# GpSimd makes the product of the gate and the state difference

## The reference

```python
h = relu(layernorm(x));  x = x + adj @ (h @ W0) + b0         # layer 0
h = relu(layernorm(x))                                       # layer 1
for _ in range(5):
    m  = adj @ h                                             # m_in = m_out, one matrix
    z  = sigmoid(m @ (w3 halves summed) + h @ u3 + biases)
    r  = sigmoid(m @ (w4 halves summed) + h @ u3 + biases)
    hv = tanh(m @ (w5 halves summed) + (r * h) @ u5 + biases)
    h  = (1 - z) * h + z * hv                                # = h + z * (hv - h)
x = x + h
```

## Time and profile before

| | |
|---|---|
| Median of 3 runs | 1661.34 us (1660.52 to 1661.93) |
| Profiled execution, its own time | 1661.44 us |
| Its span, first to last instruction | 1659.6 us |
| Mean granted TensorE clock | 0.988 of full speed |
| Busy: PE, DVE, ACT, POOL | 96%, 73%, 50%, 14% |

### The profile page before, as it was taken

How to read it: one execution, slowest core, us unless ns; L and a number is a source line. 1 busy time by engine, 2 the same in 40 slices (tenths; PEclk the granted TensorE clock), 3 DMA queues, 4 the chain that set the end, 5 groups by cost and what they waited for, 6 DMA issues and landing times.

```text
span 1659.6 us, 23908 instructions
## 1 busy us (share of the span) xinstructions
PE 1588.5 (96%) x7439; PEld 733.9 (44%) x7439; DVE 1206.0 (73%) x2311; ACT 833.9 (50%) x1298; POOL 226.4 (14%) x548
## 2 busy tenths in 40 slices
PE   5899999999999999999999999999999999999997
PEld 4444444444444444444444444444444444444443
DVE  6577677777777767776777767777768776787677
ACT  3455545455545554545545454455544555454554
POOL 4130020300213002130021201121020300200000
PEclk8999999999999999999999999999999999999998
DMA  3011111111211111111111111211111111111112
GB/s 141 26 26 36 28 39 51 32 32 29 47 38 38 25 38 38 51 25 38 25 38 51 35 28 32 59 30 32 28 35 63 25 25 38 25 38 26 38 26 51
DMA packets 179414, 63.30 MB, mean 38 GB/s; under 512 B 173504, under 2 KB 174272, under 8 KB 179392
## 3 DMA queue, kind: packets, MB, share of 16 engines
q1 hardware_dynamic: 177664, 62.43, 15.8%
q10 hardware_dynamic: 1728, 0.59, 0.1%
HBM read 13.18 MB, written 8.39 MB: 13 GB/s over the span
## 4 chain that ended last, share of the span: by engine, by line
issue 73%; POOL 12%; PE 10%; DVE 2%; DMA 1%; ACT 1%; POOLq 1%; SPq 0%; DVEq 0%
PE ps_m L503 6%; POOL y L400 4%; POOL h_lo L409 2%; DMA adj_in<-in_adj_dram 1%; POOL newton L328 1%; POOL mean L304 1%; POOL rstd L332 1%; POOL newton L318 1%; POOL var_eps L301 1%; POOL newton L330 1%; PE ps_u L510 1%; PE ps_u L512 1%; PE ps_u L511 1%; POOL gap L303 1%; POOL gap L314 0%
## 5 line engine op out<-in xcount | busy, mean ns | idle before, releaser
L503 PE MATMUL ps_m<-adj_hi,nh_hi 128*128 128x512 f16 x1536 | 584.7, 381 | 26.0 <-DVE nh_lo L897 24.4
L503 PE MATMUL ps_m<-adj_lo,nh_hi 128*128 128x512 f16 x1536 | 584.4, 380 | 0.0
L503 PE MATMUL ps_m<-adj_hi,nh_lo 128*128 128x512 f16 x1536 | 584.2, 380 | 0.0
L503 PEld LDWEIGHTS ps_m<-adj_hi,nh_hi 128*128 128x128 f16 x1536 | 150.6, 98 | 211.2 <-ACT nh_hi L670 30.5
L503 PEld LDWEIGHTS ps_m<-adj_hi,nh_lo 128*128 128x128 f16 x1536 | 150.7, 98 | 183.1 <-issue 3.3
L503 PEld LDWEIGHTS ps_m<-adj_lo,nh_hi 128*128 128x128 f16 x1536 | 150.7, 98 | 175.3 <-issue 2.0
L903 DVE SCALAR_TENSOR_TENSOR m_lo<-ps_m,m_hi 128x512 f16<-128x512 f32 x192 | 131.3, 687 | 127.4 <-ACT m_hi L705 127.4
L705 ACT ACTIVATE m_hi<-ps_m 128x512 f16<-128x512 f32 x192 | 112.3, 589 | 196.8 <-PE ps_m L503 196.8
L912 DVE SCALAR_TENSOR_TENSOR cand<-cand,h 128x512 f32<-128x512 f32 x160 | 118.6, 759 | 121.3 <-ACT cand L717 121.3
L736 ACT ACTIVATE h_hi<-h 128x512 f16<-128x512 f32 x158 | 97.3, 630 | 215.4 <-DVE h L924 215.4
L1008 DVE SCALAR_TENSOR_TENSOR rh<-ps_r,w_inv,hu 128x512 f32<-128x512 f32 x160 | 120.2, 751 | 104.8 <-PE ps_r L512 89.5
(11 more groups left out here) (134 smaller groups left out, 2003.9 us busy)
## 6 DMA issues: line engine op xcount, KB each, us to landing
x_in<-in_x_dram SPq DMA_DIRECT2D x16, 512.0 KB, 3.8
out_dram<-y SPq DMA_DIRECT2D x16, 512.0 KB, 2.7
adj_in<-in_adj_dram SPq DMA_DIRECT2D x8, 512.0 KB, 7.6
nh_hi<-h_hi SPq DMA_TRANSPOSE x128, 2.4
nh_lo<-h_lo SPq DMA_TRANSPOSE x128, 2.4
n_hi<-h_hi SPq DMA_TRANSPOSE x30, 2.4
n_lo<-h_lo SPq DMA_TRANSPOSE x30, 2.4
cand<-in_L_gnn_w_w_dram ACTq DMA_DIRECT2D x3, 128.0 KB, 6.4
```

The costliest lines, as they stand in the source:

```text
L503: last = nc.tensor.matmul(ps_m[half][:, :], a[slot][:, k, :], b[:, k, cols(half)], start=(k == 0 and n == 0), stop=(k == BLOCKS - 1 and n ...
```

## The change

The two multiplies of `new_state_end` go from DVE to POOL, in a function `gate_diff`. POOL's own loop is given up for `pair_schedule`, with `layernorm0(p + 1, 0)` put in front of `gate_diff` in `j` = `LAST`, and `layernorm0(p + 1, 1)` behind it in `j` = `LAST` - 1. `sem_inc(moment_asked, 1)` only keeps the wait ahead of it apart from the instruction behind it.

```diff
+            def gate_diff(q, slot):
+                pool.wait_ge(z_ready, q + 1)
+                for half in range(2):
+                    c = cols(half)
+                    pool.wait_ge(diff_done, 2 * q + half + 1)
+                    pool.sem_inc(moment_asked, 1)
+                    nc.gpsimd.tensor_tensor(cand[:, c], cand[:, c], z[slot][:, c], op=ALU.mult
+                                            ).then_inc(zdiff_done, 1)
+
+            def half_round(p, j, i):
+                q = n_steps(p, j, i)
+                if j == LAST and not after_all(p):
+                    layernorm0(p + 1, 0)
+                if j > 2 or (j == 0 and not before_all(p)):
+                    gate_diff(q - 1, 1 - j % 2)
+                if j in (1, 2):
+                    rest_first_h(p, j - 1)
+                if j == LAST - 1 and not after_all(p):
+                    layernorm0(p + 1, 1)
+
             layernorm0(0, 0)
             scale_weights()
             layernorm0(0, 1)
-            with pool.Fori(0, PAIRS - 1) as p:
-                for slot in range(2):
-                    rest_first_h(p, slot)
-                layernorm0(p + 1, 1)
-                layernorm0(p + 1, 0)
-            for slot in range(2):
-                rest_first_h(PAIRS - 1, slot)
+            pair_schedule(pool, half_round)
+            gate_diff(QS * PAIRS - 1, 1)
...
             def new_state_end(slot, q):
-                dve.wait_ge(z_ready, q + 1)
-                for half in range(2):
-                    c = cols(half)
-                    dve.wait_ge(diff_done, 2 * q + half + 1)
-                    nc.vector.tensor_mul(cand[:, c], cand[:, c], z[slot][:, c]).then_inc(zdiff_done, 1)
                 for half in range(2):
                     c = cols(half)
                     dve.wait_ge(zdiff_done, 2 * q + half + 1)
```

## The result

The changed kernel takes 1748.94 us (median of 4 runs, 1748.22 to 1750.02) against 1660.93 us of the kernel before on the same chip: ratio 1.053, 95% interval 1.0512 to 1.0549. It is 5.3% slower; forecast were 1742 us and 4.9%, with a range of 1715 to 1768. The profiled execution's span is 1747.4 us, 87.8 more than before, and the mean granted clock fell from 0.988 to 0.967.

A forecast was written before the change was run, and what follows sets the result against it. PE, working 1588.5 us of the span, was taken as the bound, so only its pauses count. Terms 49.7 + 15.4 + 8 + 7 + 1 = 81.1 us on a median of 1661.34 gave 1742 us, range 1715 to 1768.

The forecast's parts named there:

- PE's wait in `LAST`, less the wait for `nh_lo`: At seven pair boundaries PE stands still 9.75 us at `ps_r`, the old `nh_lo` wait goes: net 7.1 each, 49.7 us.
- `j` = 3: PE already waits 1.9 us for `m_lo` there, so the longer chain is paid in full: 8 x 1.0 = 8 us.
- `j` = 0: No slack for `m_lo` there either, so the longer chain is paid in full: 7 x 1.0 = 7 us.
- the end: The end of the program hangs on the same chain: 1 us.
- slower matmuls: PE's matmuls at the lower clock after boundary pauses: 15.4 us, bounds -4 and 24.
- The clock: Lower clock after each 9.75 us boundary pause: 7 x 2.8 - 3 x 1.4 = 15.4 us.
- The wall in `LAST`: POOL's layer norms hold up the multiplies of `LAST`, ordinary half-rounds stay covered: 1742 us, chance 0.6.
- A multiply's price: Per half-round, multiplies on POOL taking turns with DVE's adds lengthen the chain by 1.0 to 1.3 us; 1.0 taken.
- Ordinary half-rounds: The chain's extra 1.0 us is hidden under PE's `big` by a slack of 1.25 us: cost 0.
- The heavier rival: Ordinary half-rounds run out of slack too, PE waiting 0.3 us in 58 of them: 1767 us, chance 0.22.
- the lighter wall: At `LAST`, the layer norm at its floor and no fall of the clock: 1717 us, chance 0.13.
- DVE blocked by the layer norm's short instructions: Behind the multiplies of `LAST` - 1, three DVE instructions blocked up to 0.43 us each: 7 us more, if it held.

The follow-up runs named there:

- the run of both engines: A separate kernel computing nothing of the reference, timing POOL and DVE alone and together: POOL multiply alone 1.23 us, four of each together 6.77 us.
- its control: The kernel before, with each of its 316 transposing DMAs replaced by a plain DMA of the same tile: 1661.79 us, ratio 0.9999.

## Why the prediction was right, and where its sizes were off

The terms against the two profiled executions; a wait's total minus that of before:

| term | forecast, us | measured, us |
|---|---|---|
| PE's wait in `LAST`, less the wait for `nh_lo` | 49.7 | 7 x 10.18 - (24.4 - 6.4) = 53.3 |
| `j` = 3 | 8.0 | (95.4 - 71.3) - 15.4 = 8.7 |
| `j` = 0 | 7.0 | 11.4 - 2.8 = 8.6 |
| the end | 1.0 | 6.9 - 5.8 = 1.1 |
| slower matmuls (PE's busy time; see "The clock") | 15.4 | 1606.0 - 1588.5 = 17.5 |
| start of the program, not foreseen | 0 | about -1.3 |
| sum | 81.1 | 87.9 of 87.8 |

- **The wall in `LAST`** is shown by three kernels: with it and all other multiplies on POOL 1749.79, without it 1713.04, with it alone 1720.07. The forecast waited 9.75 us, PE waited 10.18. In the time of before (14.83 off) the layer norm of slot 1 ended at 426.2, not 425.1: it took 14.2 us instead of 12.7; beside DVE's adds and rests four of its first five instructions took 0.53 to 0.66 us, where later ones take 0.20. The layer norm of slot 0 took 10.8 instead of 11.3, undisturbed as DVE was waiting. The second error makes up for part of the first.
- **A multiply's price.** The chain was to grow by 1.0 us and grew by 1.11; the multiply itself takes 1.23 to 1.27 us and not 1.14, as the run of both engines shows. Turn-taking, read off 3.27 us in the earlier trace rows, held: with 1.69 us per pair, multiply, add, multiply, add need 3.4.
- **Ordinary half-rounds** stay covered, as forecast. Their `m_lo` ends at 430.01, PE starts undisturbed at 430.29, and needs 0.14 of that for the signal: 0.14 us are left of 1.25. All fifteen waits at `ps_r` are those of `j` = 3 and `LAST`. The heavier rival (1767 us) missed by this little; no run with one small POOL instruction more in each half-round shows where that edge is. There are 57 such half-rounds, not 58: the last one of all is the end.
- **`j` = 0** was undersized: it grew from 0.70 to 1.63 us, by 0.93, and it shows in all seven pairs that have it and not in four. The forecast had 7 x 1.0 and left the other three at a gain of nothing; 7 x 1.63 - 4 x 0.70 is 8.6.
- **The clock** came out near its sum by luck. Behind the 10.18 us pause PE's matmuls came every 0.43 us from 457.48 to 461.9. From that pause to the next `big` PE took 6.69 us, where the same 21 matmuls need 4.53 at the full clock: 2.2 us lost. Over the seven boundaries it is 1.5 to 2.2 us each, 12.7 together, where the forecast had 7 x 2.8 = 19.6. Less the 4.2 us of before, the boundaries cost 8.5 and not 15.4. What made up for it is a term that the forecast did not have: the lower clock also follows the pause of 3.01 us in `j` = 3, in five of eight pairs.

```profile
737.53 0.38 PE L525 MATMUL ps_r<-m_hi,w_hi 128*128 128x512 f16 x1 [3.01 <-DVE m_lo L918]
...
738.40 0.63 PE L526 MATMUL ps_u<-h_lo,w_hi 128*128 128x512 f16 x1
738.83 0.63 PE L527 MATMUL ps_u<-h_hi,w_lo 128*128 128x512 f16 x1
...
741.80 0.38 PE L525 MATMUL ps_u<-m_hi,w_hi 128*128 128x512 f16 x1
```

These five lose 1.6 to 1.7 us each, 8.3 together; 8.5 + 8.3 is 16.8 of the 17.5. Behind the waits of 1.9 us in `j` = 3 the clock never fell, neither in the kernel before nor in its control nor with only the multiplies of `LAST` on POOL; behind those of 3.0 us it fell in eight of eight pairs with the multiplies ahead of the layer norm. So `j` = 3 costs 8.7 + 8.3 = 17 us, twice the forecast.

- **What the lighter wall would have needed** was partly there, a quick layer norm of slot 0 (10.8 us), but the clock fell each time.
- **DVE blocked by the layer norm's short instructions** (7 us more, if the first to start held the shared ports for its whole instruction): not seen. DVE's rests took 1.31 us beside it instead of 1.29. The rule on the first to start stands in the Trainium skill, "SBUF — State Buffer", in the section "SBUF: two separate sides", not in the one that the prediction names. For two whole-tile instructions this case nearly agrees (1.69 us per pair, 1.84 in a row); for short instructions of POOL it does not, and the measurement decides: DVE's eight took 5.09 against 4.9 us.

What stays open is how much of the 2.6 us at the boundaries of the kernel before can be had. They come from the statistics of slot 0 being made last, at the end of `LAST` - 1, while slot 1's, which nobody needs soon, are made at `j` = 3. Exchanging the two, with the multiplies left on DVE, would give, if the boundary waits and their lower clock went altogether and the 0.7 us wait of `j` = 0 came back at the other three, 1661 - 18.4 - 4.2 + 2.1, about 1640 us. This was not run: it is an estimate, and no version that beats the kernel before is shown.

## What to carry to other kernels

An engine that is 14% busy is no free engine: what counts is what stands ahead of the moved work in its queue at the moment when it is wanted. Here fourteen multiplies behind a 10.8 us layer norm cost two thirds of the loss, and the order of two calls 37 us. Work moved off a chain's engine helps only if the chain itself gets shorter. Here 1.29 us on DVE became 1.16 us of waiting and 1.06 us of stretched adds, as both engines read two operands from SBUF and take turns. So before such a move, list the half-rounds by their slack: the same 1.1 us cost nothing in 57 of them and about its full length or more in 16. In `j` = 3 it cost about twice that, as PE's longer pause brought the lower clock behind it: price a pause with the matmuls that follow it.

## What the runs showed of the hardware that was not expected

DVE and POOL do not share their access to SBUF evenly. Against whole-tile multiplies DVE and POOL alternate one for one (four of each in 6.77 us). Against short ones DVE wins: eight DVE instructions back to back took 5.09 us with sixteen POOL `tensor_scalar` of 128x128 wanting in, and POOL got two through in 3.86 us, where ten take 4.30 us once DVE is silent. That makes a layer norm on POOL longer in the shadow of DVE, 14.2 us against 10.8, with next to nothing of it on DVE (1.31 instead of 1.29 us).

A pause of PE that grew from 1.9 to 3.0 us changed the granted clock behind it: half speed for some 3 us in 5 of 8 cases in the changed kernel and in 8 of 8 in the one with the multiplies ahead, against none of 8 before. Which further condition decides in the three pairs that kept the full clock is open.
